# A two-layer block on one core: attention units in another order, the second feed-forward net by halves of the tokens, and LoRA masks made by matrix products

## The chip, the core and the metric

The kernel runs on one core of a Trainium2 chip. TensorE (PE in the rows) does matrix products and turns, VectorE (DVE), ScalarE (ACT) and GpSimd (POOL) work beside it, and SyncE (SP) issues nearly all transfers. Each engine runs its own list of instructions in the order in which it is written, and the lists meet in semaphores. The metric is the device time of one execution in microseconds (us).

## The reference, cut to what matters

There are 1024 tokens (32 sequences of 32) of width 256. The lines touched are those of the second layer and what follows it:

```python
x1 = _ln(x) * (1.0 + scale1) + shift1
qkv = (x1 @ qkv_w + qkv_b).reshape(Bc, Tc, 3, H, DH)      # 16 heads of 128
attn = softmax(einsum(q, k) * scale)                        # within a sequence of 32
x = x + gate1 * (einsum(attn, v) @ out_w + out_b)
x2 = _ln(x) * (1.0 + scale2) + shift2
h = jax.nn.gelu(x2 @ ffn_w1 + ffn_b1, approximate=False)   # width 1024
x = x + gate2 * (h @ ffn_w2 + ffn_b2)
# LoRA experts: 8 of rank 64, each token takes the best one
probs = softmax(x_flat @ Wr.T + br); expert_weight = max(probs)
h = einsum("nd,erd->ner", x_flat, A); y = einsum("ner,eor->neo", h, B) / 64
out = y[expert_idx] * expert_weight
```

The first layer (a convolution, a causal attention and a mixture of experts) comes ahead of it and is the same in both kernels.

## The kernel before, in words

Numbers in float32 are split into a high part and a low part, and a product of two of them is three matrix products (`split_mm`, lines 1397 to 1399). ScalarE makes the high part, and VectorE or GpSimd subtracts it from the whole to give the low part. The tokens are cut into 8 tiles of 128, and into 2 halves of 512 (c is the half, 0 or 1).

**Second attention.** The work is 8 units (j, c): j is a group of 4 heads, c a half of the tokens. For each, `proj1` makes queries, keys and values with 12 products (72 instructions), `scores1` the scores, VectorE the softmax, and one unit later `pv1` and `out1` the values and the output product of each of the 4 heads. The order is (0,0), (0,1), (1,0), (1,1), (2,0), (2,1), (3,0), (3,1). Each group has 4 pieces of weights (queries, keys, values, output), 16 in all, which go by SyncE into one of 4 raw buffers, by ScalarE (`piece_hi`, 128x1024) and GpSimd (`piece_lo`) into one of 6 slots. A piece is read in by the units of both halves.

**Between attention and the second net.** Since the last two units are (3,0) and (3,1), both halves of the output are complete only at the end. Then, for each half: VectorE adds the gated output to x (`residual2`), TensorE turns x into token rows (`turn_x2`, L1723), ScalarE copies it, VectorE normalises it, TensorE turns it back (`turn_z2`, L1740), VectorE applies scale and shift, and ScalarE and GpSimd split it. TensorE fills part of this time with turns of a constant that nobody reads (`keep_warm`, L1438): 22 ahead of the last `pv1`, 4, 8, 8 and 18 between the turns of half 0, and 14 behind the first product of the net.

**Second net.** 8 slices (m) of width 128, for each of the 2 halves: `ffn_up` (6 instructions) makes 128x512 of hidden values, ScalarE takes the Gelu (L933) and the high part (L937), VectorE the low part (`hidden_lo`, L1294), and `ffn_down` (6 instructions) adds to the output. The list `FFN` has three slices of half 0, three of half 1, two slices with both halves, and then three and three again. The weights of a slice go through one of 3 raw buffers (SyncE), `slice_hi` (ScalarE) and `slice_lo` (GpSimd).

**LoRA and the end.** When the net is done, x is complete and `logits1` gives the router's 8 logits (L1822). `lora_up` makes the hidden values of two experts at a time (8 products of 6 instructions, L1397 to L1399). The router's choice, with its share, is turned (`turn_sel`, L1830), copied by ScalarE, written to DRAM, and read back by SyncE so that each of 64 rows holds the mask of its expert. VectorE multiplies (L1379), `lora_down` (L1852) sums over experts, VectorE adds x (L1371), and 8 transfers write the output.

## Time and profile before

| | us |
|---|---|
| median of 3 runs | 650.28 |
| lowest and highest of the 3 | 649.84, 653.76 |
| the profiled execution, as timed | 652.73 |
| its span, first to last instruction | 650.6 |
| TensorE busy in it | 611.8 |

The profile is of one execution. Its span is 2.1 us less than its own time. A busy TensorE is not a TensorE that does useful work: the turns of `keep_warm` count as busy, and so does a product at the lower clock. In the timeline a group of like instructions is one row, and what stands in brackets is the idle time of the engine ahead of it and what ended it. A matrix product of 128x512 at the full clock is shown with 0.39 us, of which a part overlaps the next one: they start about 0.227 us apart.

### The profile page before, as it was taken

Reading aid. Unit: us, or ns where it says so; the run is one execution under the profiler, and the core shown is the slowest. Engines: PE = TensorE matmul, PEld = TensorE weight load, DVE = VectorE, ACT = ScalarE, POOL = GpSimd, SP = SyncE. Lnnn points to the kernel's source line nnn. Section 1 sums busy time; section 2 is a strip of 40 time slices with the busy share of each in tenths; the row PEclk is TensorE's granted clock in tenths of the full one; section 3 lists DMA queues with packets and bytes.
Section 4 is the critical chain, followed back from the end, with each engine's and each line's share of the span. In section 5 each row is a group of like instructions: output and inputs, shape, how many; then the busy total and the mean of one; then the engine's idle time right before and its main releaser. Section 6 shows DMA issues by size and latency. Waiting matters only on the chain.

```text
span 650.6 us, 13581 instructions
## 1 busy us (share of the span) xinstructions
PE 611.8 (94%) x5578; PEld 514.3 (79%) x5578; DVE 380.8 (59%) x672; ACT 339.2 (52%) x855; POOL 199.0 (31%) x214
## 2 busy tenths in 40 slices
PE   4679999999999999999899999999999999789997
PEld 1668888888888788888787887888888887668776
DVE  2689779777885665884844525153261437842553
ACT  2586677866876544542355553453544343445440
POOL 0566344354446314540333221040130013532000
PEclk9588999999999999999999999999999999989999
DMA  8460000000000247443002021020000002100023
GB/s 276 182 250 20 1 2 3 3 2 2 1 3 27 95 163 198 138 147 113 2 1 66 8 91 33 3 65 2 1 1 2 0 2 66 32 17 17 0 68 129
DMA packets 13101, 36.27 MB, mean 56 GB/s; under 512 B 2256, under 2 KB 3792, under 8 KB 12432
## 3 DMA queue, kind: packets, MB, share of 16 engines
q1 hardware_dynamic: 12800, 34.36, 16.2%
q10 hardware_dynamic: 240, 1.05, 0.6%
q8 instruction: 44, 0.72, 0.5%
q14 instruction: 17, 0.14, 0.1%
HBM read 34.29 MB, written 1.11 MB: 54 GB/s over the span
## 4 chain that ended last, share of the span: by engine, by line
PE 79%; DVE 11%; ACT 5%; issue 2%; DMA 2%; POOL 1%; SPq 0%; DVEq 0%; ACTq 0%
PE ps L1397 19%; PE ps L1398 18%; PE ps L1399 18%; PE ps L1515 7%; PE ps L1694 4%; PE ps L1474 2%; PE ps L1852 2%; DMA xT<-in_x_T 2%; ACT hid L671 2%; PE ps L1682 1%; PE ps L1504 1%; PE ps L1492 1%; PE ps L1426 1%; DVE strm_lo L1264 1%; ACT strm_hi L880 1%
## 5 line engine op out<-in xcount | busy, mean ns | idle before, releaser
L500 POOL TENSOR_TENSOR w_lo<-raw_w,w_hi 128x1024 fp32r<-128x1024 f32 x20 | 48.9, 2462 | 143.3 <-ACT w_hi L640 121.0
L1264 DVE SCALAR_TENSOR_TENSOR strm_lo<-ps,col,strm_hi 128x512 fp32r<-128x512 f32 x32 | 24.0, 751 | 113.9 <-ACT strm_hi L880 112.7
L1397 PE MATMUL ps<-w_hi,act_hi 128*128 128x512 f32 x160 | 65.7, 411 | 5.2 <-ACT junk L633 3.6
L864 ACT ACTIVATE work<-ps,col 128x512 f32<-128x512 f32 x64 | 44.2, 690 | 49.0 <-PE ps L1399 48.9
L1397 PE MATMUL ps<-act_hi,w_hi 128*128 128x512 f32 x160 | 62.9, 393 | 1.8 <-POOL act_lo L588 1.2
L1398 PE MATMUL ps<-w_lo,act_hi 128*128 128x512 f32 x160 | 63.6, 397 | 0.0
L1399 PE MATMUL ps<-w_hi,act_lo 128*128 128x512 f32 x160 | 63.4, 396 | 0.0
L1399 PE MATMUL ps<-act_hi,w_lo 128*128 128x512 f32 x160 | 62.3, 390 | 0.0
L1398 PE MATMUL ps<-act_lo,w_hi 128*128 128x512 f32 x160 | 62.3, 389 | 0.0
L1515 PE MATMUL ps<-raw_w,xT 128*128 128x256 f32 x256 | 61.3, 380 | 0.0
L1515 PEld LDWEIGHTS ps<-raw_w,xT 128*128 128x128 f32 x256 | 46.3, 190 | 5.3
L633 ACT ACTIVATE junk<-ps 128x128 f32<-128x128 f32 x160 | 43.9, 337 | 0.0
L1397 PE MATMUL ps<-act_hi,strm_hi 128*128 128x512 f32 x104 | 42.0, 404 | 0.0
L1398 PE MATMUL ps<-act_lo,strm_hi 128*128 128x512 f32 x104 | 41.4, 398 | 0.0
L1397 PEld LDWEIGHTS ps<-w_hi,act_hi 128*128 128x128 f32 x160 | 30.9, 193 | 13.2 <-issue 5.8
L1399 PE MATMUL ps<-act_hi,strm_lo 128*128 128x512 f32 x104 | 41.1, 395 | 0.0
L1397 PE MATMUL ps<-w_hi 128*128 128x256 f32 (+1 forms) x120 | 38.3, 319 | 2.3 <-DVE w_lo L1294 1.6
L633 ACT ACTIVATION_READ_ACCUMULATOR junk<-ps 128x1 f32 x160 | 40.0, 271 | 0.0
L1399 PE MATMUL ps<-w_hi,w_lo 128*128 128x256 f32 (+1 forms) x120 | 38.1, 317 | 0.0
L1398 PE MATMUL ps<-w_lo,w_hi 128*128 128x256 f32 (+1 forms) x120 | 37.9, 316 | 0.0
L714 ACT ACTIVATE work<-ps 128x512 f32<-128x512 f32 x40 | 24.1, 620 | 25.9 <-PE ps L1474 25.9
L1397 PEld LDWEIGHTS ps<-act_hi,w_hi 128*128 128x128 f32 x160 | 30.0, 188 | 8.3 <-issue 1.6
(192 smaller groups left out, 1458.4 us busy)
## 6 DMA issues: line engine op xcount, KB each, us to landing
raw_w<-in_w_attn SPq DMA_DIRECT2D x16, 512.0 KB, 4.2
raw_s<-in_w_moe SPq DMA_DIRECT2D x11, 384.0 KB, 5.5
work<-comb_dram SPq DMA_DIRECT2D x21, 128.0 KB, 2.9
raw_w<-in_w_qkv SPq DMA_DIRECT2D x4, 512.0 KB, 12.6
raw_w<-in_w_o SPq DMA_DIRECT2D x1, 2048.0 KB, 8.0
work<-comb_dram SPq DMA_DIRECT2D x8, 256.0 KB, 5.1
raw_s<-in_w_ffn SPq DMA_DIRECT2D x8, 256.0 KB, 2.6
bd<-in_w_ada SPq DMA_DIRECT2D x1, 1536.0 KB, 6.5
```

What stands on the lines that cost most here:

```text
L500: G.tensor_tensor(flat(w_lo[:, slot]), raw, flat(f32(w_hi[:, slot])), ALU.subtract).then_inc(s_piece_lo, 1)
L633: A(junk[:, squares[0] % 3, 0:n], src, ACT.Square, accum_out=total).then_inc(s_squares, 1)
L671: A(*conv_out(q, b, tiles), ACT.Copy).then_inc(s_y_act, 1)
L714: A(qkT[:, k * BANK:(k + 1) * BANK], ps[:, QK_BANK[k], :], ACT.Copy).then_inc(s_qkT_copied, 1)
L864: A(dst[:, h * BANK:(h + 1) * BANK], src, ACT.Identity, bias=c_(b, 4 * j + h)).then_inc(s_q1_copied, 1)
L1264: V.scalar_tensor_tensor(flat(strm_lo[:, n % SS]), ps[:, 4 + n % 2, :], c_("bv", 4 * (u // CHUNKS) + h), flat(f32(strm_hi[:, n % SS])), AL ...
L1397: mm(dst, ah, bh, start=start and i == 0, stop=False, **flags)
L1398: mm(dst, ah, bl, start=False, stop=False, **flags)
L1399: last = mm(dst, al, bh, start=False, stop=stop and i == len(terms) - 1, **flags)
L1474: last = nc.tensor.transpose(ps[:, QK_BANK[k], h * DH:(h + 1) * DH], qr[:, k * BANK + h * DH:k * BANK + (h + 1) * DH], ident)
L1515: mm(ps[:, 7, 0:D], attnT[:, h * P:(h + 1) * P], wo0[:, h, :], start=(h == 0), stop=(h == HQ - 1)).then_inc(s_o0_head, 1)
L1694: last = mm(ps[:, 4 + n % 2, t * P:(t + 1) * P], v1[:, u % 2, t, h * DH:(h + 1) * DH], bd[:, u % 2, 4 * h + t].rearrange("p b q -> p (b q) ...
```

## The change

The units of the attention are taken in the order (0,0), (0,1), (1,0), (1,1), (2,0), (3,0), (3,1), (2,1), so half 0 is complete one whole unit earlier. Group 2 is no longer done in one go, so its 4 pieces are loaded and split a second time (20 pieces instead of 16; `PIECES` is the first piece of a unit). The turns of half 0, its norm and its split are done beside the last unit's `proj1`, and the turned tiles lie in `hid`. `FFN` is now all slices of half 0 and then all of half 1. Two of its `ffn_up` stand ahead of the last unit's `pv1`, and the turns of half 1 stand among the products of half 0. The `keep_warm` calls there are gone, but for one of 8 turns between the halves. The first `logits1` stands within the second half of the net.

For the LoRA masks the transfers through DRAM are gone. VectorE writes once a constant of 8x128 for each pair of experts (`expand`), and a matrix product of it with the turned choice (`selT`) gives the mask in PSUM (`mask1`, one 128x512 instruction each, 8 in all). The share of the expert is now multiplied in where the result is added to x (`add_lora`, by tiles of 128 tokens).

TensorE, from the end of the loop over the units; before (L1438 is `keep_warm`, L1694 `pv1`, L1723 `turn_x2`, L1740 `turn_z2`):

```order
L1438 MATMUL ps<-cst 128x128 x22
L1694 MATMUL ps<-bd,work 128x128 [waits pv1_lo,bd1,q1_copied]
...
L1723 MATMUL ps<-cst,xT 128x128 [waits x2_ready,s1_shifted]
L1723 MATMUL ps<-cst,xT 128x128 x3
...
L1740 MATMUL ps<-cst,work 128x128 [waits z2_ready,q1_copied]
...
L1438 MATMUL ps<-cst 128x128 x4
```

and now (L1469 is the first instruction of a `split_mm`, those that read `strm_hi` belong to `out1` and those that read `act_hi` here to `ffn_up`; L1772 is `pv1`):

```order
L1469 MATMUL ps<-strm_hi,w_hi 128x512
...
L1469 MATMUL ps<-act_hi,w_hi 128x512 [waits xn3_ready,slice_lo]
...
L1469 MATMUL ps<-act_hi,w_hi 128x512 [waits s1_shifted,xn3_ready,slice_lo]
...
L1772 MATMUL ps<-bd,work 128x128 [waits pv1_lo,bd1,q1_copied]
...
L1772 MATMUL ps<-bd,work 128x128 [waits pv1_lo]
...
L1469 MATMUL ps<-strm_hi,w_hi 128x512 [waits acc1,piece_lo,pv1_lo]
...
L1772 MATMUL ps<-bd,work 128x128 [waits pv1_lo]
```

The filler is gone, and two products of the net stand ahead of the last unit's values.

TensorE, inside `proj1` of the last unit, now (L1813 is `turn_x2`, L1830 `turn_z2`; before there was nothing between the products here):

```order
L1469 MATMUL ps<-act_hi,w_hi 128x512 [waits q1_copied,piece_lo]
...
L1813 MATMUL ps<-cst,xT 128x128 [waits s1_shifted,x2_ready]
L1813 MATMUL ps<-cst,xT 128x128
L1469 MATMUL ps<-act_hi,w_hi 128x512 [waits q1_copied]
...
L1813 MATMUL ps<-cst,xT 128x128 [waits x2_ready]
...
L1469 MATMUL ps<-w_hi,act_hi 128x512 [waits q1_copied,piece_lo]
...
L1830 MATMUL ps<-cst,hid 128x128 [waits acc1,z2_ready]
L1830 MATMUL ps<-cst,hid 128x128
L1469 MATMUL ps<-w_hi,act_hi 128x512 [waits q1_copied]
```

The turns of half 0 stand ahead of the products 5 to 11, and the first waits for `x2_ready`, which VectorE gives.

ScalarE, behind the last exponent's unit, before (L647 is `slice_hi`, L880 the copy of `pv1`, L917 the copy of `turn_x2`):

```order
L647 ACTIVATE w_hi<-raw_s 128x512 [waits ld_slice0,out1,proj1]
...
L647 ACTIVATE w_hi<-raw_s 128x512 [waits ld_slice0]
L880 ACTIVATE strm_hi<-ps,col 128x512 [waits out1,pv1] x4
L917 ACTIVATE work<-ps 128x256 [waits x2T] x4
L647 ACTIVATE w_hi<-raw_s 128x512 [waits ld_slice1,out1]
L647 ACTIVATE w_hi<-raw_s 128x512 [waits ld_slice2]
...
L933 ACT_TABLE_LOAD
```

and now (L652 is `slice_hi`, L934 the Gelu, L944 the high part, L902 the copy of `pv1`):

```order
L950 ACT_TABLE_LOAD
...
L652 ACTIVATE w_hi<-raw_s 128x512 [waits ld_slice2,proj1]
L652 ACTIVATE w_hi<-raw_s 128x512 [waits ld_slice0]
L652 ACTIVATE w_hi<-raw_s 128x512 [waits ld_slice1]
L652 ACTIVATE w_hi<-raw_s 128x512 [waits ld_slice2]
L934 ACTIVATE work<-ps,col 128x512 [waits ffn_up]
L944 ACTIVATE w_hi<-work 128x512 [waits out1,gelu]
L902 ACTIVATE strm_hi<-ps,col 128x512 [waits out1,pv1] x2
```

The copies of the last unit's `pv1` stood behind four slices before. Now the table load, four slices, the first Gelu and its high part stand ahead of the first two of them.

The diff, cut to its core:

```diff
         g32 = v1_[:, 0:2 * BANK].rearrange("p (r n) -> p r n", r=2)
-        cb1 = work[:, 0:4 * TOK].rearrange("p (r n) -> p r n", r=MR)
         h1 = bd[:].rearrange("p r a b c -> p (r a b c)").rearrange("p (r n) -> p r n", n=BANK)
 
+        selT = w_hi2[0:NE, 2:4, :]
...
@@ -337,7 +339,11 @@
         QK_BANK = (2, 3, 0, 1, 2)
         Y_FIRST, Y_REST = slice(0, 2), slice(2, TILES)
         U = GROUPS * CHUNKS
-        NP1 = 4 * GROUPS
+        UNITS = ((0, 0), (0, 1), (1, 0), (1, 1), (2, 0), (3, 0), (3, 1), (2, 1))
+        PIECES = (0, 0, 4, 4, 8, 12, 12, 16)
+        LAST_UNIT = (1, 3, 4, 6)
+        NP1 = 4 * GROUPS + 4
+        C0_DONE = 6
         NM = CHUNKS * MI
         NF = CHUNKS * MM
...
         Z_BEHIND = (4, 6, 8, 10)
 
-        FFN = ([(m, c) for c in range(CHUNKS) for m in range(SS)]
-               + [(m, c) for m in range(SS, MM - SS) for c in range(CHUNKS)]
-               + [(m, c) for c in range(CHUNKS) for m in range(MM - SS, MM)])
+        FFN = [(m, c) for c in range(CHUNKS) for m in range(MM)]
+        SLICE_SLOT = (2, 4, 5, 0)
+        HIDDEN = (6, 7, 2, 3)
+        Z2_BANK = (6, 7, 3, 6, 6, 7, 6, 7)
+        X2_BEHIND = (5, 6, 7, 8)
+        Z2_BEHIND = (9, 10, 11)
+
+        def up_bank(n):
+            return 3 - n % 2 if n < MM else 4 + n % 4
+
...
-            u = CHUNKS * j + CHUNKS - 1
+            u = LAST_UNIT[j]
...
+                sp.dma_start(raw_p[:, i % RAWS, :], w_attn1[i if i < 4 * GROUPS else i - 8]).then_inc(ld_piece[i % RAWS], 16)
...
-            for c in range(CHUNKS):
-
-                s = slice(c * BANK, (c + 1) * BANK)
-                sp.wait_ge(s_selT_ready, c + 1)
-                sp.dma_start(comb_dram[1, :, s], selT[0:NE, s]).then_inc(st_comb, 16)
-                sp.wait_ge(st_comb, 16 * (CHUNKS + c + 1))
-                for n in range(c * MR, (c + 1) * MR):
-                    m = LORA[n][0]
-                    spread(cb1[:, m, s], 1, m, RANK, ld_cb1[n], s)
             for t in range(TILES):
-                sp.wait_ge(s_y_ready, t // 2 + 1)
+                sp.wait_ge(s_y_ready, t + 1)
...
                 piece_lo(NPROJ + i, raw_p[:, i % RAWS, :], i % WSLOTS)
-            def mod2(c):
+            for f in range(2):
+                slice_lo(MI + f, f, 4)
+            for c in range(CHUNKS):
                 for t in range(c * CT, (c + 1) * CT):
                     pool.wait_ge(s_ln2st, t + 1)
                     inv_root(stat[:, 40 + t:41 + t], bst[:, t, 7:8], 1, 1.0, 1e-6, s_l2rstd)
                 for t in range(c * CT, (c + 1) * CT):
                     mod_lo(TILES + t, t, mt2[:, t % 4, :], s_xn3_ready)
-
-            for f in range(4):
-                slice_lo(MI + f, f, 4)
-            mod2(0)
-            slice_lo(MI + 4, 4, 4)
-            slice_lo(MI + 5, 5, 4)
-            mod2(1)
-            for f in range(6, MM):
-                slice_lo(MI + f, f, 4)
+                if c == 0:
+                    for f in range(2, MM):
+                        slice_lo(MI + f, f, 4)
...
+                    if u == U - 1:
+                        if k in (2, 3):
+                            act.wait_ge(s_proj1, 12 * (U - 1))
+                            slice_hi(MI + k - 2, k - 2, 4)
+                        if k in X2_BEHIND:
+                            take_x2(X2_BEHIND.index(k))
+                        if k in Z2_BEHIND[1:]:
+                            mod2_hi(Z2_BEHIND.index(k) - 1)
...
+            TAKEN = ((), (6, 7, 8), (9,), (10, 11, 12), (13, 14, 15), (16, 17), (18, 19), ())
...
+                for i in TAKEN[u]:
+                    used_sem, count = piece_free(i)
+                    act.wait_ge(used_sem, count)
+                    piece_hi(NPROJ + i, i % RAWS, i % WSLOTS)
...
+            A(junk[:, 0, 0:1], half[:, 0:1], ACT.Gelu)
+            act.wait_ge(s_proj1, 12 * U)
+            for f in range(2, 6):
+                slice_hi(MI + f, f, 4)
+            take_ffn(0)
+            take_pv1(U - 1, (0, 1))
+            take_ffn(1)
+            take_pv1(U - 1, (2, 3))
+            for f in range(6, MM):
+                slice_hi(MI + f, f, 4)
+            take_ffn(2)
+            take_ffn(3)
+            for t in range(CT, TILES):
+                take_x2(t)
+            take_ffn(4)
+            take_ffn(5)
...
-
-            x4_hi(0)
+                act.wait_ge(s_ffn_down, NF)
+                A(selT[:, c, :], ps[0:NE, c, :], ACT.Copy).then_inc(s_selT_ready, 1)
...
-                dve.wait_ge(s_acc1, DK * (U - CHUNKS + c + 1))
+                dve.wait_ge(s_acc1, DK * (C0_DONE if c == 0 else U))
...
+                if u == C0_DONE:
+                    residual2(0, range(DK))
+                    for t in range(CT + 2):
+                        if t < CT:
+                            stats2(t)
+                        if 1 <= t <= CT:
+                            apply2(t - 1)
+                        if t >= 2:
+                            modulate2(t - 2)
+            hidden_lo(0)
+            low_heads(U - 1, (0, 1))
+            hidden_lo(1)
+            low_heads(U - 1, (2, 3))
+            add_out(U - 1)
             residual2(1, range(DK))
-            norm2(1)
-
-            for n in range(2, NF):
-                hidden_lo(n)
-
-            def router1(c):
+            stats2(4)
+            stats2(5)
+            hidden_lo(2)
+            apply2(4)
+            stats2(6)
+            apply2(5)
+            hidden_lo(3)
+            stats2(7)
+            apply2(6)
+            modulate2(4)
+            apply2(7)
+            modulate2(5)
+            modulate2(6)
+            hidden_lo(4)
+            modulate2(7)
...
+            def end_ffn(c):
+                dve.wait_ge(s_ffn_down, MM * (c + 1))
                 for m in range(DK):
                     gated(ps[:, 2 * c + m, :], 5, "b2", c, m).then_inc(s_x4_ready, 1)
...
+            for n in range(5, NF):
+                hidden_lo(n)
+                if n == MM:
+                    dve.wait_ge(s_out1, 4 * U)
+                    for m in range(MR):
+                        V.tensor_copy(expand(m).rearrange("p (e r) -> p e r", e=2),
+                                      over(ident[0:NE, 2 * m:2 * m + 2], RANK)).then_inc(s_expand, 1)
+                if n == MM + 1:
+                    end_ffn(0)
+                if n == MM + 3:
+                    x4_lo(0)
+                if n == MM + 6:
+                    router_shift(0)
+            router_probs(0)
+            end_ffn(1)
+            router_pick(0)
+            x4_lo(1)
+            router_shift(1)
+            router_probs(1)
+            router_pick(1)
+
...
-                for a in range(c * CT // 2, (c + 1) * CT // 2):
-                    t2 = slice(2 * a, 2 * a + 2)
-                    V.tensor_tensor(xres[:, t2, :], ps[:, (a + 2) % 4, :].rearrange("p (b n) -> p b n", b=2),
-                                    xres[:, t2, :], ALU.add).then_inc(s_y_ready, 1)
+                dve.wait_ge(s_share, c + 1)
+                for t in range(c * CT, (c + 1) * CT):
+                    V.scalar_tensor_tensor(xres[:, t, :], ps[:, (t // 2 + 2) % 4, (t % 2) * D:(t % 2 + 1) * D],
+                                           rt[:, 6, t, 0:1], xres[:, t, :], ALU.mult, ALU.add).then_inc(s_y_ready, 1)
...
-                dve.wait_ge(ld_cb1[n], 32)
+                dve.wait_ge(s_mask1, n + 1)
                 if n >= 3:
                     dve.wait_ge(s_hmk_used, n - 2)
-                V.tensor_tensor(hmk[:, n % 3, :], h1[:, n, :], cb1[:, m, c * BANK:(c + 1) * BANK],
+                V.tensor_tensor(hmk[:, n % 3, :], h1[:, n, :], ps[:, 4 + n % 4, :],
...
+                    if u == U - 1 and k in X2_BEHIND:
+                        turn_x2(X2_BEHIND.index(k))
+                    if u == U - 1 and k in Z2_BEHIND:
+                        turn_z2(Z2_BEHIND.index(k))
                     n = 12 * u + k
-                    i = 4 * j + k // 4
+                    i = PIECES[u] + k // 4
...
-            def turn_x2(c):
-                pe.wait_ge(s_x2_ready, DK * (c + 1))
...
+            ffn_up(0)
+            ffn_up(1)
+            pv1(U - 1, 0)
+            pv1(U - 1, 1)
+            out1(U - 1, 0)
+            pv1(U - 1, 2)
+            out1(U - 1, 1)
+            pv1(U - 1, 3)
+            out1(U - 1, 2)
+            out1(U - 1, 3)
+            ffn_up(2)
+            ffn_down(0)
+            ffn_up(3)
+            turn_x2(4)
+            turn_x2(5)
+            ffn_down(1)
+            turn_x2(6)
+            turn_x2(7)
+            ffn_up(4)
+            ffn_down(2)
+            turn_z2(4)
+            turn_z2(5)
+            ffn_up(5)
+            ffn_down(3)
+            turn_z2(6)
+            turn_z2(7)
+            ffn_up(6)
+            ffn_down(4)
+            ffn_up(7)
+            ffn_down(5)
+            ffn_down(6)
+            ffn_down(7)
+            keep_warm(8, 5)
+            ffn_up(8)
+            ffn_up(9)
+            for n in range(10, NF):
+                ffn_up(n)
+                ffn_down(n - 2)
+                if n == NF - 3:
+                    logits1(0)
+            ffn_down(NF - 2)
+            ffn_down(NF - 1)
+
...
+            def mask1(n):
+                m, c = LORA[n]
+                if n == 0:
+                    pe.wait_ge(s_expand, MR)
+                pe.wait_ge(s_selT_ready, c + 1)
+                pe.wait_ge(s_up_copied, MR + n % MR + 1)
+                if c == 1:
+                    pe.wait_ge(s_hmk_ready, n - MR + 1)
+                mm(ps[:, 4 + n % 4, :], expand(m), selT[:, c, :],
+                   start=True, stop=True).then_inc(s_mask1, 1)
 
...
             for n in range(NL):
                 if n == 2:
                     logits1(1)
-                if n == 3:
+                if n == MR:
                     turn_sel(0)
-                if n == MR + 1:
-                    turn_sel(1)
                 lora_up(n)
-            for n in range(MR):
-                lora_down(n)
-            pe.wait_ge(s_selT_ready, CHUNKS)
-            for n in range(MR, NL):
+                if n >= NL - 2:
+                    mask1(n - NL + 2)
+            turn_sel(1)
+            mask1(2)
+            lora_down(0)
+            mask1(3)
+            for n in range(1, NL):
+                if n + MR - 1 < NL:
+                    mask1(n + MR - 1)
                 lora_down(n)
 
```

## Rows read from the trace of the kernel before

**Rows 1.** The page: busy time, share of the span, instructions.
```profile
PE 611.8 (94%) x5578; PEld 514.3 (79%) x5578; DVE 380.8 (59%) x672; ACT 339.2 (52%) x855; POOL 199.0 (31%) x214
```
**Rows 2.** Timeline, TensorE, 509 to 574: start, duration, line, tiles, count, [idle <-releaser].
```profile
509.54 0.40 PE L1397 MATMUL ps<-act_hi,w_hi 128*128 128x512 f32 x1
...
536.85 2.56 PE L1438 MATMUL ps<-cst 128*128 128x128 f32 x22
...
540.00 2.02 PE L1694 MATMUL ps<-bd,work 128*128 128x128 f32 x16 [0.58 <-issue]
...
542.69 0.50 PE L1397 MATMUL ps<-strm_hi,w_hi 128*128 128x512 f32 x1 [0.67 <-DVE strm_lo L1264]
...
551.71 0.41 PE L1740 MATMUL ps<-cst,work 128*128 128x128 f32 x2
...
558.73 0.47 PE L1397 MATMUL ps<-act_hi,w_hi 128*128 128x512 f32 x1 [0.62 <-POOL act_lo L588]
...
563.50 0.66 PE L1723 MATMUL ps<-cst,xT 128*128 128x128 f32 x4 [1.62 <-DVE xT L1283]
...
570.14 0.44 PE L1740 MATMUL ps<-cst,work 128*128 128x128 f32 x2 [0.69 <-DVE work L1218]
...
572.13 0.50 PE L1397 MATMUL ps<-w_hi 128*128 128x512 f32 x1 [1.55 <-DVE w_lo L1294]
...
573.20 0.63 PE L1397 MATMUL ps<-w_hi 128*128 128x512 f32 x1
```
**Rows 3.** Timeline, TensorE, from the dense second feed-forward net to the end.
```profile
576.58 0.39 PE L1397 MATMUL ps<-act_hi,w_hi 128*128 128x512 f32 x1
...
613.07 0.39 PE L1399 MATMUL ps<-w_hi,w_lo 128*128 128x512 f32 x1
...
614.33 1.95 PE L1822 MATMUL ps<-r_w,xT 128*128 128x8 f32 x16 [0.87 <-DVE xT L1283]
...
617.28 0.63 PE L1398 MATMUL ps<-act_lo,strm_hi 128*128 128x512 f32 x1
...
627.59 0.60 PE L1830 MATMUL ps<-cst,rt 128*8 128x128 f32 x4 [0.51 <-DVE rt L1350]
...
632.14 13.97 PE L1852 MATMUL ps<-raw_s,work 128*128 128x256 f32 x64
```
**Rows 4.** Timeline, VectorE, the attention units and behind the last.
```profile
426.48 2.28 DVE L1064 TENSOR_TENSOR sm_e<-sm_e,sm_r 128x512 f32<-128x512 f32 x1
...
509.63 2.90 DVE L1078 STREAM_TRANSPOSE bd<-sm_e 32x512 f32<-32x512 f32 x4
...
512.56 1.29 DVE L1275 TENSOR_TENSOR yT<-ps,yT 128x512 f32<-128x512 f32 x2
...
558.54 1.84 DVE L1281 SCALAR_TENSOR_TENSOR yT<-yT,col,ada 128x512 f32<-128x512 f32 x1
...
561.98 0.74 DVE L1281 SCALAR_TENSOR_TENSOR yT<-yT,col,ada 128x512 f32<-128x512 f32 x1
```
**Rows 5.** Timeline, GpSimd, in the same two stretches.
```profile
425.80 7.57 POOL L500 TENSOR_TENSOR w_lo<-raw_w,w_hi 128x1024 fp32r<-128x1024 f32 x3 [22.63 <-ACT w_hi L640]
...
558.54 2.97 POOL L507 TENSOR_TENSOR w_lo<-raw_s,w_hi 128x512 fp32r<-128x512 f32 x2
```
**Rows 6.** Timeline, ScalarE, the attention units and behind the last.
```profile
454.99 1.06 ACT L640 ACTIVATE w_hi<-raw_w 128x1024 fp32r<-128x1024 f32 x1 [2.53 <-PE ps L1399]
...
539.00 0.63 ACT L647 ACTIVATE w_hi<-raw_s 128x512 fp32r<-128x512 f32 x1 [2.92 <-DMA raw_s<-in_w_ffn]
...
565.57 1.28 ACT L933 ACT_TABLE_LOAD   x1
```
**Rows 7.** Timeline, SyncE's queue.
```profile
536.44 23.75 SPq L468 DMA_DIRECT2D raw_s<-in_w_ffn  x5
```
**Rows 8.** Groups by line and shape, 340 to the end: busy, mean ns, idle before.
```profile
L1379 DVE TENSOR_TENSOR work<-bd,work 128x512 f32<-128x512 f32 x8 | 5.5, 692 | 8.6 <-DMA work<-comb_dram 8.1 <-ACT bd L963 0.5
...
L933 ACT ACTIVATE work<-ps,col 128x512 f32<-128x512 f32 x16 | 11.0, 688 | 18.7 <-PE ps L1399 16.7 <-DVE w_lo L1294 2.0
```

More of the change, by code:

```diff
@@ L331, in build_program @@
         s_wsel = sem("wsel")
+        s_expand = sem("expand")
+        s_share = sem("share")
         s_hmk_ready = sem("hmk_ready")
@@ new lines, in _ @@
+            pe.wait_ge(s_x1_ready, 1)
+            for t in range(CT):
+                keep_warm((14, 14, 6, 14)[t], 0)
+                turn_z(t)
+            keep_warm(16, 0)
+            pe.wait_ge(s_x1_ready, 2)
+            for u in range(U):
+                proj1(u)
+                if u == 1:
+                    pe.wait_ge(s_xn1_ready, TILES)
+                    pe.wait_ge(s_xT1_copied, TILES)
+                if u == U - 1:
+                    turn_z2(CT - 1)
+                if u >= 1:
+                    pv1(u - 1, 0)
+                    pv1(u - 1, 1)
+                if u == 0:
+                    pe.wait_ge(s_x1_ready, 4)
+                scores1(u)
+                if u >= 1:
+                    out1(u - 1, 0)
+                    pv1(u - 1, 2)
+                    out1(u - 1, 1)
+                    pv1(u - 1, 3)
+                    out1(u - 1, 2)
+                    out1(u - 1, 3)
```

354 lines of the change are left out of this document (150 added, 204 removed).

## The prediction

> **What bounds the kernel now.** I read the page's busy times first. TensorE is busy for 611.8 of 650.6 us [rows 1], so it sets the pace, and a gain must come from time in which it waits, turns a filler, or runs at its lower clock. The timeline of TensorE was next. Ahead of 536.85 each unit of the attention takes 27.3 us without a gap worth naming: the last unit's `proj1` starts at 509.54 and the filler behind that pass of the loop at 536.85 [rows 2]. The second net is dense from 576.58 to 613.3; between the rows 576.58 and 613.07 lie 161 steps, 0.227 us each [rows 3], so a `split_mm` of 6 instructions is 1.36 us. Between 536.85 and 576.58, and around 614, the time is not dense, and the change works there. ScalarE, VectorE, GpSimd and SyncE are read only for what they would make TensorE wait for.
>
> **What goes.** All in TensorE's time:
> - the 22 filler turns and the idle time behind them, 536.85 to 540.00: 3.15. The wait ahead of 542.69: 0.7 [rows 2].
> - 551.71 to 558.73 is 7.0, in which the four tiles of `turn_z2` are work, 0.25 each (a filler turn is 2.56 / 22 = 0.12 and a tile takes two): 6.0 goes [rows 2].
> - the first `ffn_up` of 558.73 ends its six steps at 560.1, and the turn behind it starts at 563.50: 3.4 [rows 2].
> - 563.50 to 572.13 is 8.6; two `ffn_up` (2.7), four `turn_x2` tiles at 0.33 (two are 0.66) and four `turn_z2` tiles are work, 5.0 together: 3.6 goes [rows 2].
> - the lower clock behind this: 572.13 to 576.58 holds 12 steps and takes 4.45 instead of 2.7. A product of 128x512 is 0.63 there and 0.39 when dense [rows 2, 3], so the granted clock is at its lower level of 1.2 GHz, after a stretch in which TensorE waited for 0.69 and 1.55 with only turns around it: 1.7.
> - ahead of the LoRA part 0.9 of idle time at 614.33, and the same dip after it (0.63 again at 617.28): 1.7. Now the first `logits1` stands inside the net, where it costs what it cost (it only moves). The wait ahead of the second turned choice at 627.59: 0.5 [rows 3].
>
> Together 21.7. The turns of half 0, four of each kind, move and cost the same.
>
> **What comes.**
> - 8 mask products of 128x512, single instructions, 8 x 0.227 = 1.8. Filler of 8 turns: 0.9.
> - The mask transfers bring nothing back. VectorE waits for them for 8.1 us in sum [rows 8], but from 614.33 on TensorE's only idle time is the 0.5 counted above, and the 64 records of `lora_down` run for 13.97 without a break [rows 3]. The share moves from a multiply at the router to the last sum, which becomes 8 instructions of 256 columns for 4 of 512: nothing on the path beyond some tenths.
> - Between units 4 and 5 ScalarE now has three pieces in a row (13, 14, 15), and the first waits for the end of `out1`, as the piece at 454.99 did (1.06 each, released by TensorE) [rows 6]. 3.2 of pieces and 0.69 for the first copy put the third product of `proj1` off to 4.0 from 2.7: 1.3.
> - **The first turn of half 0** stands ahead of product 5 of the last `proj1`, at 6.8 behind its start S. VectorE must by then have ended the turns of the softmax (509.63 and 2.90) and `add_out` (512.56 and 1.29), which is S + 4.3 [rows 2, 4], and then two pairs of `residual2`. A pair is 0.74 and about 0.69 (the mean of L1379, of the same size), so both are 2.9 and ready at S + 7.2: a stall of 0.4, the low end. But GpSimd now splits pieces 18 and 19 (about 2.5 each, three are 7.57) and slices 0 and 1 at that time. With GpSimd at work the softmax product at 426.48 took 2.28, and `residual2` at 558.54 took 1.84 where it takes 0.74 alone [rows 4, 5]. If all of it is stretched so (1.6, and 2.0 for a pair), it is ready at S + 10.8: 4.0, the high end. Slice 1 is done by about S + 6.8, soon after `residual2` starts at S + 5.9 (4.3 and the first stretch of 1.6), so I take the first stretch whole and a third of the second: 2.7.
>
>   The Trainium skill ("SBUF — State Buffer", section on SBUF's two separate sides) states that VectorE with two SBUF inputs and GpSimd hold a shared port for a whole instruction and the other blocks. By that rule the stall would be the rest of slice 1 and no more, 2.7 again and not 4.0, and a stretch by a factor, as the bare rows could be read, would give 4.0. The rows fit it: 558.54 is the start of both.
> - **Behind the last pass**, at E. ScalarE loads its table (1.28 at 565.57), which now is at E - 2.3 to E - 1.0, and then takes slices 2 to 5, before the copies of `pv1`. Slice 5 needs a buffer that GpSimd frees by slice 2, near E + 1.1, and a transfer, which took 2.56 from the issue at 536.44 to its use at 539.00 [rows 6, 7]: E + 3.7. With the copy of slice 5 (0.63), the Gelu (0.69), its high part (0.63) and the copy of `pv1` (0.69) ScalarE is at E + 6.3, and VectorE's low part at E + 7.1 [rows 6, 8]. TensorE has two `ffn_up` (2.7) and two `pv1` (2.0) to do until E + 4.7: 2.4 of idle time. At the low end, with the slice in time, it is 0.3.
> - These two stalls stand where TensorE is otherwise dense. Each is longer than the 1.55 that had a dip behind it, and the fillers are gone. I count one dip of 1.7 for the two (none to two are the ends).
> - Handing over among turns, `residual2` of half 1 and the low parts: VectorE has about 15 us of work in a row there against some 14 of products, and each low part is ready 0.5 to 2 us before it is needed by my count: 1.0.
>
> Sum: 1.8 + 0.9 + 1.3 + 2.7 + 2.4 + 1.7 + 1.0 = 11.8 come and 21.7 go: -9.9. The profiled execution would go from 652.7 to 642.8 (span 640.7). It lay 2.4 above the median of the runs, so the median would be 650.3 - 9.9 = **640.4**.
>
> **Rivals.**
> 1. *The new waits are covered.* The piece, the residual and the slice are in time or nearly (low ends: 1.3 less 0.8, 2.7 less 2.3, 2.4 less 2.1) and no dip follows (1.7): 640.4 - 6.9 = 633.5. For it: with piece 19 split earlier than I think VectorE runs alone, and 4 us between S and the first turn are then nearly enough. Against it: the pairs of rows 4 and 5. Chance 0.18.
> 2. *VectorE becomes late throughout the first half of the net.* Two dips, the residual at its high end and 3 more of waiting for low parts: 640.4 + 1.7 + 1.3 + 3 = 646.4. For it: the order puts norms ahead of the low parts. Chance 0.14.
> 3. *The masks do give back their wait*: if the LoRA part is held by VectorE's 8.1 us, it is 632. Against it stands the unbroken row of 13.97. Chance 0.02.
> 4. *Slower*: the first half of the net falls into step with its Gelu. Only two banks serve its `ffn_up`, so when a low part comes later than its `ffn_down`, product n + 2 waits for n as well, and each of the 8 slices pays Gelu, high and low part one behind the other: 0.69 + 0.63 + 0.69 + 0.2 for handing on = 2.2, 17.6 in sum: 658. It decides once VectorE is more than a slice (2.7) behind; my count leaves 0.7 ahead at the third low part. Chance 0.04.
>
> The forecast has 0.62. **Range** 633.5 to 647: it reaches rival 1 and rival 2, and leaves out rivals 3 and 4 and the tails, under 0.2. A change of less than 1% (6.5 us, so 643.8 to 656.8) can't be told from none here. The forecast with nearly all of its chance, and rivals 1 and 3, are faster by more: 0.86; rival 2 and the forecast's upper tail are within: 0.10; rival 4 slower: 0.04.
>
> **What would show it.** In the changed profile: no `keep_warm` of 22, the span about 10 shorter. An idle time of 1 to 1.5 ahead of the third product of unit 5's `proj1`, released by ScalarE. One of 2 to 3 ahead of the first `turn_x2`, released by VectorE's xT; if it is 0.5, rival 1. About 2.4 ahead of the last unit's first `out1`, released by the low part; behind one of them some products at 0.63. A net of some 60 us from the end of the loop to its last product. `lora_down` without waits for masks. I am wrong if TensorE waits within the net for `w_lo` again and again, or if a stall sits where I named none: the first places to look are the pieces 16 to 19 and the buffers of the slices.

## The result

| | before | changed |
|---|---|---|
| median of 14 runs each, us | 652.84 | 647.75 |
| lowest and highest | 649.84, 655.25 | 641.88, 651.39 |
| the profiled execution, as timed | 652.73 | 647.96 |
| its span | 650.6 | 646.2 |

The ratio is 0.9909 (95% interval 0.9884 to 0.9934): 0.9% faster, 5.1 us on the medians, where 9.9 was forecast. That is less than the 1% which was said to be hard to tell from none, but the interval leaves 1 out. 647.75 lies 0.75 above the range. Part of the distance to 640.4 is the base: the median of the three runs shown was 650.28, that of all 14 is 652.84. The rest, 4.8 us, is a matter of the kernel.

The first line of the changed kernel's page answers to [rows 1]. TensorE is busy for 3.4 us less, and still for 94% of the span:

```profile
PE 608.4 (94%) x5520; PEld 509.0 (79%) x5520; DVE 381.9 (59%) x680; ACT 342.0 (53%) x860; POOL 207.9 (32%) x218
```

TensorE's timeline of the changed kernel, the waits and what follows them. L1469 to L1471 are the three products of a `split_mm`, L1813 is `turn_x2`, L1800 `logits1`. A stretch of products shown with 0.63 for 0.39 is called a *dip* from here on: TensorE's granted clock is at its lower level in it.

```profile
459.52 0.50 PE L1469 MATMUL ps<-act_hi,w_hi 128*128 128x512 f32 x1 [0.90 <-ACT work L884]
...
521.54 0.64 PE L1813 MATMUL ps<-cst,xT 128*128 128x128 f32 x2 [2.61 <-DVE xT L1322]
...
522.41 0.63 PE L1470 MATMUL ps<-act_lo,w_hi 128*128 128x512 f32 x1
...
552.76 0.50 PE L1469 MATMUL ps<-strm_hi,w_hi 128*128 128x512 f32 x1 [2.04 <-DVE strm_lo L1303]
...
576.14 0.50 PE L1469 MATMUL ps<-w_hi 128*128 128x512 f32 x1 [0.78 <-DVE w_lo L1333]
...
610.78 1.95 PE L1800 MATMUL ps<-r_w,xT 128*128 128x8 f32 x16 [0.31 <-DVE xT L1322]
...
613.85 0.63 PE L1471 MATMUL ps<-act_hi,strm_lo 128*128 128x512 f32 x1
```

All three forecast waits are there, with the releasers forecast and nearly the sizes: 0.90 (I had 1.3), 2.61 (2.7), 2.04 (2.4). What had gone in the old region (the 22 fillers, the waits and turns of [rows 2]) is gone. What is missing from the gain is at the end. `mask1` is L1958 and `lora_down` L1968; TensorE's timeline, then its weight loads (PEld) of the first two rows:

```profile
621.36 0.39 PE L1471 MATMUL ps<-act_hi,strm_lo 128*128 128x512 f32 x1
621.68 0.50 PE L1958 MATMUL ps<-w_hi,strm_hi 8*128 8x512 f32 x1
622.11 0.50 PE L1469 MATMUL ps<-act_hi,strm_hi 128*128 128x512 f32 x1
622.44 0.39 PE L1470 MATMUL ps<-act_lo,strm_hi 128*128 128x512 f32 x1
...
627.00 0.73 PE L1958 MATMUL ps<-w_hi,strm_hi 8*128 8x512 f32 x2
627.66 2.00 PE L1968 MATMUL ps<-raw_s,work 128*128 128x256 f32 x8
629.59 0.50 PE L1958 MATMUL ps<-w_hi,strm_hi 8*128 8x512 f32 x1
630.01 2.00 PE L1968 MATMUL ps<-raw_s,work 128*128 128x256 f32 x8
631.94 0.50 PE L1958 MATMUL ps<-w_hi,strm_hi 8*128 8x512 f32 x1
...
634.71 7.17 PE L1968 MATMUL ps<-raw_s,work 128*128 128x256 f32 x32
```

```profile
621.14 0.19 PEld L1471 LDWEIGHTS ps<-act_hi,strm_lo 128*128 128x128 f32 x1
621.68 0.18 PEld L1958 LDWEIGHTS ps<-w_hi,strm_hi 8*128 8x128 f32 x1 [0.35 <-issue]
622.10 0.19 PEld L1469 LDWEIGHTS ps<-act_hi,strm_hi 128*128 128x128 f32 x1 [0.25 <-issue]
```

Read the starts, not the durations. Two products of 128 rows start 0.227 us apart. Here the mask product starts 0.32 after the one ahead of it, the next one 0.43 after it, and the one behind that 0.33 later: 1.08 for three steps that take 0.68 elsewhere, so 0.40 more. And the weight load of a 128-row product runs 0.22 ahead of its product (621.14 for 621.36), while that of the mask product starts with it, and so does the next one. A mask with its eight `lora_down` takes 2.35 (629.59 to 631.94), where eight alone take 1.74 (64 take 13.97 in [rows 3]). The masks were forecast at 0.227 each.

### The profile page after: what moved, and what is told of

Read it like the earlier page. It is cut to its first block, busy times and chain, and to the rows that moved or that the text cites. A ratio compares the mean times of both kernels' runs of the same rounds, so it can differ in the third digit from the quotient of the medians.

```text
span 646.2 us, 13493 instructions
## 1 busy us (share of the span) xinstructions
PE 608.4 (94%) x5520; PEld 509.0 (79%) x5520; DVE 381.9 (59%) x680; ACT 342.0 (53%) x860; POOL 207.9 (32%) x218
## 3 DMA queue, kind: packets, MB, share of 16 engines
HBM read 34.29 MB, written 1.08 MB: 55 GB/s over the span
## 4 chain that ended last, share of the span: by engine, by line
PE 81%; DVE 8%; ACT 5%; issue 2%; DMA 2%; POOL 1%; SPq 0%; DVEq 0%; ACTq 0%
PE ps L1469 19%; PE ps L1471 18%; PE ps L1470 18%; PE ps L1587 7%; PE ps L1772 4%; PE ps L1546 3%; PE ps L1968 2%; DMA xT<-in_x_T 2%; PE ps L1564 2%; ACT hid L676 2%; PE ps L1760 1%; PE ps L1576 1%; PE ps L1623 1%; DVE strm_lo L1303 1%; PE ps L1498 1%
## 5 line engine op out<-in xcount | busy, mean ns | idle before, releaser
L509 POOL TENSOR_TENSOR w_lo<-raw_w,w_hi 128x1024 fp32r<-128x1024 f32 x24 | 58.5, 2457 | 160.7 <-ACT w_hi L645 139.0
L1303 DVE SCALAR_TENSOR_TENSOR strm_lo<-ps,col,strm_hi 128x512 fp32r<-128x512 f32 x32 | 23.9, 750 | 103.1 <-ACT strm_hi L902 102.1
L1469 PE MATMUL ps<-w_hi,act_hi 128*128 128x512 f32 x160 | 66.3, 414 | 4.6 <-ACT junk L638 3.2
L1469 PE MATMUL ps<-act_hi,w_hi 128*128 128x512 f32 x160 | 64.2, 401 | 2.0 <-ACT work L884 0.9
L1471 PE MATMUL ps<-w_hi,act_lo 128*128 128x512 f32 x160 | 63.8, 399 | 0.0
L1471 PE MATMUL ps<-act_hi,w_lo 128*128 128x512 f32 x160 | 62.9, 393 | 0.0
L1469 PE MATMUL ps<-act_hi,strm_hi 128*128 128x512 f32 x104 | 41.8, 402 | 0.0
L1471 PE MATMUL ps<-act_hi,strm_lo 128*128 128x512 f32 x104 | 41.3, 397 | 0.0
L1469 PEld LDWEIGHTS ps<-w_hi,act_hi 128*128 128x128 f32 x160 | 31.0, 194 | 12.4 <-issue 5.4
L1469 PE MATMUL ps<-w_hi 128*128 128x256 f32 (+1 forms) x120 | 37.8, 315 | 1.5 <-DVE w_lo L1333 0.8
L1471 PE MATMUL ps<-w_hi,w_lo 128*128 128x256 f32 (+1 forms) x120 | 37.4, 312 | 0.0
L1469 PEld LDWEIGHTS ps<-act_hi,w_hi 128*128 128x128 f32 x160 | 30.5, 191 | 8.7 <-ACT work L884 1.3
```

The lines of the kernel that those rows point to most:

```text
L509: G.tensor_tensor(flat(w_lo[:, slot]), raw, flat(f32(w_hi[:, slot])), ALU.subtract).then_inc(s_piece_lo, 1)
L1303: V.scalar_tensor_tensor(flat(strm_lo[:, n % SS]), ps[:, 4 + n % 2, :], c_("bv", 4 * UNITS[u][0] + h), flat(f32(strm_hi[:, n % SS])), ALU. ...
L1469: mm(dst, ah, bh, start=start and i == 0, stop=False, **flags)
L1471: last = mm(dst, al, bh, start=False, stop=stop and i == len(terms) - 1, **flags)
```

## The experiments

Each was timed in turn with the kernel before on one chip, and ratios are against that. There were three sets: the kernel before had 654.82, 654.18 and 653.73 in them. In the first set the question was where the missing 4.8 us are: A, in the masks; B, in the reordering.

**The masks alone, in the kernel before.**

```
-                dve.wait_ge(ld_cb1[n], 32)
+                dve.wait_ge(s_mask1, n + 1)
...
-                V.tensor_tensor(hmk[:, n % 3, :], h1[:, n, :], cb1[:, m, c * BANK:(c + 1) * BANK],
+                V.tensor_tensor(hmk[:, n % 3, :], h1[:, n, :], ps[:, 4 + n % 4, :],
```

> The kernel before with one part of the change alone: masks by 8 products, share at the last sum; the order of units and of the net as before. Theory A (a mask product costs 0.63 on TensorE, product and changeover, as the spacing of 0.43 plus a longer lora_down beside it in the changed kernel's trace suggests): 8 x 0.63 = 5.0 more, 0.5 of waiting for the second choice less, so 4 to 5 us slower than the kernel before. Theory B (it costs its 0.23, as predicted, and the LoRA part of the changed kernel is long only by its dip in the clock): 1 to 2 us slower. Rival C (the mask transfers did hold the LoRA part): faster by 3 or more.

657.21 us, ratio 1.0037 (1.0008 to 1.0067): 2.4 us slower, with the interval from 0.5 to 4.4. In its trace a mask product starts 0.42 ahead of its successor, as in the changed kernel (0.43):

```profile
631.23 0.50 PE L1850 MATMUL ps<-w_hi,strm_hi 8*128 8x512 f32 x1
631.65 0.50 PE L1394 MATMUL ps<-act_hi,strm_hi 128*128 128x512 f32 x1
```

From the first `logits1` to the end of the last `lora_down` it takes 35.62 (615.80 to 644.25 + 7.17) where the kernel before takes 31.78 (614.33 to 646.11): 3.84 longer. So the mask half of the change is a loss by itself, on the time as well, though the time lies between the two theories (A: 4 to 5 slower, B: 1 to 2).

**The transfers back, in the changed kernel.**

```
+                sp.dma_start(comb_dram[1, :, s], selT[0:NE, s]).then_inc(st_comb, 16)
...
+                    spread(cb1[:, m, s], 1, m, RANK, ld_cb1[n], s)
...
-                mm(ps[:, 4 + n % 4, :], expand(m), selT[:, c, :],
-                   start=True, stop=True).then_inc(s_mask1, 1)
```

> The changed kernel with the masks sent through DRAM again; all else of the change kept. Theory A: the 5.0 of the products go, and the transfers cost some 2 of waiting, since the choice is turned no earlier against the products: 2 to 4 us faster than the changed kernel, ratio to before near 0.987. Theory B: 1.8 go and 2 of waiting come: the same as the changed kernel. Rival C: slower than the changed kernel by 3 or more, lora_down held by the transfers.

644.80 us, ratio 0.9845 (0.9806 to 0.9884). The transfers are the better way against masks of 8 rows, though TensorE now does wait for VectorE twice:

```profile
623.64 7.17 PE L1961 MATMUL ps<-raw_s,work 128*128 128x256 f32 x32 [0.66 <-DVE work L1455]
631.27 7.14 PE L1961 MATMUL ps<-raw_s,work 128*128 128x256 f32 x32 [0.45 <-DVE work L1455]
```

These 1.1 us are all that VectorE's waits for transfers are worth to TensorE: 8.6 us in this trace (8.1 in [rows 8]).

**Mask products over 128 rows.** The 8 rows are padded by rows of zeros that lie there anyway; the number of products, their columns and their order stay.

```
-        selT = w_hi2[0:NE, 2:4, :]
-        expand = lambda m: strm_hi[0:NE, m // 2, 2 + m % 2, :]
+        selT = w_hi2[:, 2:4, :]
+        expand = lambda m: strm_hi[:, m // 2, 2 + m % 2, :]
...
```

> The changed kernel with the mask products summed over 128 rows of which 120 are zeros, instead of over 8 rows. If the changeover between an 8-row product and the 128-row ones around it is what costs (A1), the spacing from a mask to the next product falls from 0.43 to about 0.23 to 0.3 and the kernel is 2 to 3 us faster than the changed one. If the cost lies in going between the single-instruction format and the two-record float32 products (A2), spacing and time stay as they are.

642.66 us, ratio 0.9830 (0.9787 to 0.9872). Sixteen times as many rows, and it is faster. TensorE's timeline and its loads:

```profile
618.45 0.39 PE L1471 MATMUL ps<-act_hi,strm_lo 128*128 128x512 f32 x1
618.67 0.39 PE L1958 MATMUL ps<-w_hi,strm_hi 128*128 128x512 f32 x1
618.90 0.39 PE L1469 MATMUL ps<-act_hi,strm_hi 128*128 128x512 f32 x1
...
624.87 0.58 PE L1958 MATMUL ps<-w_hi,strm_hi 128*128 128x512 f32 x1
625.29 1.89 PE L1968 MATMUL ps<-raw_s,work 128*128 128x256 f32 x8
626.83 0.58 PE L1958 MATMUL ps<-w_hi,strm_hi 128*128 128x512 f32 x1
```

```profile
618.45 0.19 PEld L1958 LDWEIGHTS ps<-w_hi,strm_hi 128*128 128x128 f32 x1
618.68 0.19 PEld L1469 LDWEIGHTS ps<-act_hi,strm_hi 128*128 128x128 f32 x1
```

Now the load is at 618.45 for the product at 618.67, and a mask costs 0.227, or 1.95 with its eight `lora_down` (624.87 to 626.83). So it isn't the product that is slow, it is the change between 8 and 128 rows. From 0.991 to 0.983 is more than the rows account for: some 5 us, of which the masks are 2.7 (the table below). This trace also lacks the dip behind the first turn; the rest lies within the intervals.

**Other row counts**, 32 and 64, one execution each and read from the trace alone (`w_hi2[0:32, ...]` and `w_hi2[0:64, ...]` in the lines above).

> The changed kernel with the mask products over 32 rows (24 of them zero) instead of 8. Read from the trace alone, since one time says nothing here. Theory A1 (any product that uses fewer than the 128 rows pays when its row count differs from its neighbour's): the distance from a mask product to the next instruction stays 0.43 us and the group of 8 lora_down behind it about 1.93. Theory A2 (only very few rows are slow, for instance because the operands come from few partitions): the distance is between 0.43 and 0.227.

> The same over 64 rows (56 of them zero). A1: again 0.43 us and 1.93. A2: nearer to 0.227 than with 32 rows.

With 64 rows the picture is that of 8, to the hundredth, and with 32 too (0.43 from 626.68 to 627.11):

```profile
621.20 0.39 PE L1471 MATMUL ps<-act_hi,strm_lo 128*128 128x512 f32 x1
621.52 0.50 PE L1958 MATMUL ps<-w_hi,strm_hi 64*128 64x512 f32 x1
621.95 0.50 PE L1469 MATMUL ps<-act_hi,strm_hi 128*128 128x512 f32 x1
```

A1 holds: any of the row counts 8, 32 and 64 pays the same among products of 128.

**Filler in the two late places.**

```
+                    if u == U - 1 and k == X2_BEHIND[0]:
+                        keep_warm(22, 3)
                     if u == U - 1 and k in X2_BEHIND:
                         turn_x2(X2_BEHIND.index(k))
...
             pv1(U - 1, 1)
+            pe.wait_ge(s_q1_copied, 12 * U)
+            keep_warm(16, 0)
             out1(U - 1, 0)
```

> The changed kernel with 22 filler turns ahead of the first turn of x2 in the last proj1 and 16 ahead of the last unit's first out1, in the two places where TensorE waits 2.61 and 2.04 in its trace. If the dip in the clock behind 521.8 comes of that wait (theory D), it is gone in the trace (no 128x512 product of 0.63 there), and the time is 1 to 2 us under the changed kernel's. If dips come by themselves (rival E), there is one all the same and the time is the same.

646.05 us, ratio 0.9867 (0.9828 to 0.9906). TensorE has no product at the lower clock anywhere behind the start of the attention in this execution. The filler stands in the time of the waits and ends neither sooner. So I put the gain, about 3 us against the changed kernel, down to the dips: behind the two waits there are 1.3 of them on average (counted below), about 2.1 us. The interval is too wide to tell 2.1 from 3.

**The changed kernel once more**, in the second set.

> The changed kernel once more, with nothing edited, beside the others of this set, so that they can be compared on one chip. Both theories: 0.991 of the kernel before, as in the first comparison (interval 0.988 to 0.993), so about 649 us if the kernel before is again at 654.8. In its trace the rows of the attention and of the LoRA part as before: first turn_x2 2.6 us late, out1 of the last unit 2.0 late, each mask product of 8 rows 0.43 us ahead of the next instruction. Whether a stretch at the lower clock (0.63 us per 128x512 product) follows the late turn and the second logits may differ: in the five traces so far it followed the late turn in 2 of 4 and the logits in 4 of 6.

649.75 us, ratio 0.9915 (0.9887 to 0.9943). In this execution there are dips in three places, one more than in the first: 5 rows at 0.63 behind the first turn, 3 behind the last unit's first `out1`, 7 behind `logits1`.

**Slice 5 later on ScalarE.**

```
-            for f in range(2, 6):
+            for f in range(2, 5):
                 slice_hi(MI + f, f, 4)
             take_ffn(0)
             take_pv1(U - 1, (0, 1))
+            slice_hi(MI + 5, 5, 4)
             take_ffn(1)
```

> The changed kernel, ScalarE's split of slice 5 moved behind the copies of the last unit's first two pv1. Theory A (the 2.04 us ahead of the last unit's first out1 come from slice 5, whose transfer ends late and which stands ahead of the copy on ScalarE): the first copy starts at about 1 us behind the first pv1, the low part 0.7 later, and the idle time falls to 0.8 or less: 1.2 to 1.5 us shorter than the changed kernel, about 0.989. Rival B (VectorE's own list, Gelu low parts and turns of the softmax, holds the low part): the idle time stays at 2 and the time too, 0.991.

643.69 us, ratio 0.9828 (0.9797 to 0.9858). The wait is 0.67 now:

```profile
552.13 0.50 PE L1470 MATMUL ps<-strm_hi,w_hi 128*128 128x512 f32 x1 [0.67 <-DVE strm_lo L1304]
```

From the last `pv1` to the second `logits1` it takes 60.69 (549.43 to 610.12), the first execution of the changed kernel 62.08 (548.70 to 610.78) without a dip there, and the second 63.73 (550.17 to 613.90) with one. So 1.39 is the wait, as theory A said, and 1.65 is the dip, which the shorter wait did not show. The medians differ by 6.1, more than those two. The profiled execution has no dip behind `logits1` either (1.6), and the mean granted clock is 0.979 over the five executions, for 0.969 over the six of the changed kernel beside it, which points to fewer dips in this version. Why the one behind `logits1` would be rarer is open.

**The turns of half 0 two products later.**

```
-        X2_BEHIND = (5, 6, 7, 8)
-        Z2_BEHIND = (9, 10, 11)
+        X2_BEHIND = (7, 8, 9, 10)
+        Z2_BEHIND = (11,)
...
```

The other three `turn_z2` go behind `proj1`, among `pv1(6, 0)` and `pv1(6, 1)`.

> The changed kernel, the four turn_x2 of half 0 two products later in the last proj1 (ahead of products 7 to 10 instead of 5 to 8), turn_z2 0 ahead of product 11 and the other three behind proj1 and among the two pv1. Theory A (the residual is ready 9.45 us behind the start of this proj1, two products later the turn finds it ready): the 2.6 us ahead of the first turn go, 0.5 to 1.5 come back behind it, since VectorE starts the softmax of the last unit later by so much: 1 to 2 us shorter than the changed kernel, and the stretch at the lower clock that followed in 2 of 4 traces (1.7 us) not there: 0.987 to 0.989. Rival B (the norm is the bound up to the end of the loop): the same 2.6 us show up ahead of out1 or pv1 instead: 0.991.

645.29 us, ratio 0.9860 (0.9832 to 0.9887). The first turn waits for nothing any more; half of it comes back one step on, where `out1` waits for the norm's last step:

```profile
535.64 0.47 PE L1475 MATMUL ps<-strm_hi,w_hi 128*128 128x512 f32 x1 [1.25 <-DVE work L1273]
```

Between the same two points (511.37 to 546.58) it takes 35.21 and the changed kernel beside it 38.26 (511.91 to 550.17): 1.4 less waiting and one dip less.

**All mends together**: 128 rows, slice 5, the turns, and the fourth weight piece of group 3 taken inside the next `proj1` instead of as the third in a row.

```
+                    if u == 5 and k == 3:
...
+                        piece_hi(NPROJ + 15, 15 % RAWS, 15 % WSLOTS)
...
-            TAKEN = ((), (6, 7, 8), (9,), (10, 11, 12), (13, 14, 15), (16, 17), (18, 19), ())
+            TAKEN = ((), (6, 7, 8), (9,), (10, 11, 12), (13, 14), (16, 17), (18, 19), ())
```

> The changed kernel with every mend at once: mask products over 128 rows (120 of them zero), slice 5 later, the turns of half 0 later, and the fourth weight piece of group 3 taken inside the next proj1 instead of as the third of three in a row (its 0.9 us of idle time ahead of the third product go). If the parts add up: 2.7 (masks) + 1.3 + 1.5 + 0.9 = 6.4 us less than the changed kernel, and about one stretch at the lower clock less: 0.979 to 0.982 of the kernel before. If the masks' width was not the cause of what was measured before (0.983), no better than 0.985.

640.15 us, ratio 0.9767 (0.9737 to 0.9796), 9.6 us less than the changed kernel beside it. More than the 6.4 of the parts and one dip, 8.1, though within the intervals.

**And the second logits in two parts**, with the former once more beside it in the third set:

```
-                if n == 2:
-                    logits1(1)
+                if n in (2, 3):
+                    logits1(1, 2 * (n - 2), 2 * (n - 1))
...
                 lora_up(n)
```

The two numbers added to `logits1` are the first tile and the one behind the last.

> The version with all four mends once more, with nothing edited, beside the next one: 0.977 of the kernel before (interval 0.974 to 0.980 at first).

> The version with all four mends, and logits1 of half 1 in two parts of 8 short products, with one lora_up between them. Theory D (the stretch at the lower clock behind it, 1.7 us in 7 of 10 traces, comes from TensorE having 0.3 us of idle time and 1.8 us of short products in a row): the stretch is gone or rarer, 0.5 to 1.7 us less than the version with four mends, the choice of half 1 comes 1.4 us later and still in time (it was ready 2.7 early). Rival (it comes whatever stands there): the stretch shows in the trace as before, no difference.

639.18 us, ratio 0.9770 (0.9738 to 0.9802), and 637.32 us, ratio 0.9747 (0.9718 to 0.9776). The wait of 0.31 stays and no dip follows: none of the products between the two parts and behind them is at 0.63.

```profile
606.10 1.06 PE L1811 MATMUL ps<-r_w,xT 128*128 128x8 f32 x8 [0.31 <-DVE xT L1331]
...
608.26 0.39 PE L1482 MATMUL ps<-act_hi,strm_lo 128*128 128x512 f32 x1
608.50 0.95 PE L1811 MATMUL ps<-r_w,xT 128*128 128x8 f32 x8
```

The medians differ by 1.9, the size of a dip, with intervals that overlap. One trace without the dip shows little (3 of 11 had none with `logits1` in one piece), but the mean granted clocks point the same way: 0.981 on average over these six executions, and 0.976 over the twelve with the four mends alone. This last version beats both kernels: 2.5% less than before.

**The LoRA part over all traces.** One length settles the two terms: from the start of the second `logits1` to the end of the last `lora_down`. A dip is seen by 6 to 8 rows at 0.63.

| mask products | dip | traces | us | one of them |
|---|---|---|---|---|
| 8, 32 or 64 rows | yes | 5 | 31.06 to 31.10 | 610.78 to 641.88, the changed kernel |
| 8 rows | no | 2 | 29.48, 29.51 | 609.67 to 639.15, with filler |
| 128 rows | yes | 3 | 28.37 to 28.39 | 606.65 to 635.02, all mends |
| 128 rows | no | 1 | 26.79 | 606.10 to 632.89, logits in two |
| transfers | no | 1 | 26.58 | 611.83 to 638.41 |

The four corners fit one another: changing rows costs 2.7 with a dip (31.07 less 28.37) and 2.7 without (29.49 less 26.79), and a dip costs 1.6 with either. The masks alone in the kernel before fit too: 1.8 and 2.7, less the wait of 0.5 that goes, are 4.0, and 3.84 was measured. And the last two rows say what the mask products are worth: with 8 rows they cost 2.9 more than the transfers, and with 128 rows still 0.2 more, in one trace each. No version of them was shown to beat the transfers.

## Why the prediction was wrong

The direction was right, and the reordering half came in full: from the first product of the attention to the last of the net it takes 281.6 us (325.74 to 607.37) for 289.3 (323.75 to 613.07), 7.7 less, where the terms of the prediction give 6.9 less with the first `logits1` (1.7) moved in. From there to the last `lora_down` it takes 34.5 for 33.0: 1.5 more, where 3.0 less was forecast. Two terms in this part were wrong. Against the profiled execution (652.73 to 647.96, so -4.8 where -9.9 was forecast) 5.1 is missing.

- **The step that failed: "8 mask products of 128x512, single instructions, 8 x 0.227 = 1.8".** They measure 4.5: the table's 2.7 on top of 1.8, which is about 0.40 for each of the 7 places where rows change (629.59 to 631.94 is 2.35, less the 1.95 with 128 rows), the two masks in a row counting once (0.66 for both at 627.00). I took the price from the shape of the output and never looked at "8x512", nor at the weight loads, which have lines of their own. The trace of before had the answer. In the first layer a product of 32 rows (L1504) stands among those of 128, and the starts are 0.32 apart, with the load not ahead:

```profile
82.53 0.39 PE L1399 MATMUL ps<-w_hi,act_lo 128*128 128x512 f32 x1
82.85 1.17 PE L1504 MATMUL ps<-pT,work 32*128 32x128 f32 x32
83.95 0.50 PE L1397 MATMUL ps<-w_hi,act_hi 128*128 128x512 f32 x1
```

```profile
82.85 0.98 PEld L1504 LDWEIGHTS ps<-pT,work 32*128 32x128 f32 x32 [0.35 <-issue]
```

  The Trainium skill ("TensorE: Matmul & The Clock Gate", the section on loading the stationary operand) states that the time of a weight load goes by its columns and not by its rows. The rows agree: 0.18 for 8x128, 0.19 for 128x128. So the cost isn't in the load's length; what goes with it is the load's place.
- **The second step that failed: "ahead of the LoRA part 0.9 of idle time at 614.33, and the same dip after it: 1.7".** The dip was counted as gone. The idle time is gone but for 0.31, the dip isn't. It moved to the second `logits1`, which waits only 0.31 and is then 1.8 us of products with 8 columns. Of the 11 traces of the changed kernel and its variants with `logits1` in one piece 8 have the dip: 1.6 missing in the profile. With the logits in two parts it was gone in the one trace there is.
- **2.0 us lie ahead of all that was changed**: the first product of the attention starts at 325.74 here and at 323.75 in the profile of before. Executions differ so in this stretch with one and the same program: in other traces of the changed kernel's variants, which are equal up to there, that product starts at 323.54 to 327.23, and at 325.23 in the kernel before with the masks alone. TensorE's clock goes with it: up to this product it is at the lower level for 27.3 us in the changed kernel's profile, for 23.9 in that of before and in the one that starts at 323.54. So these 2.0 us belong to the pair of executions and not to the kernel.
- **The waits that come** were a little smaller than forecast (0.4, 0.1 and 0.4), which gives back 0.9. Hand-overs within the net: 0.78 at 576.14 and the 0.31 above, for 1.0. 2.7 + 1.6 + 2.0 - 0.9 is 5.4, against 5.1.
- **For the medians** 4.8 is missing. The masks are 2.7, the dip behind `logits1` 1.2 on average (8 of 11), the dips behind the two waits 0.4 more than the 1.7 counted, and the smaller waits give back 0.9: 3.4. The other 1.4 is open; the interval of the ratio is 3.3 us wide.
- **The first turn at 2.7** came out at 2.61, where the bare stretch by a factor would have given 4.0. VectorE's two operations beside GpSimd, in its timeline:

```profile
511.33 2.27 DVE L1099 TENSOR_TENSOR sm_e<-sm_e,sm_r 128x512 f32<-128x512 f32 x1
513.64 2.91 DVE L1113 STREAM_TRANSPOSE bd<-sm_e 32x512 f32<-32x512 f32 x4
...
517.90 1.47 DVE L1320 SCALAR_TENSOR_TENSOR yT<-yT,col,ada 128x512 f32<-128x512 f32 x1
519.41 0.69 DVE L1322 TENSOR_TENSOR xT<-xT,yT 128x512 f32<-128x512 f32 x1
520.02 0.74 DVE L1320 SCALAR_TENSOR_TENSOR yT<-yT,col,ada 128x512 f32<-128x512 f32 x1
```

```profile
510.65 5.22 POOL L509 TENSOR_TENSOR w_lo<-raw_w,w_hi 128x1024 fp32r<-128x1024 f32 x2 [22.10 <-ACT w_hi L645]
516.17 2.65 POOL L516 TENSOR_TENSOR w_lo<-raw_s,w_hi 128x512 fp32r<-128x512 f32 x2 [0.30 <-ACT w_hi L652]
```

  The same operation takes 1.47 while GpSimd's slice runs until 518.82, and 0.74 at 520.02 when it doesn't; the turns with one input take 2.91 as always. One operation is held in each of the two stretches, not all of them, and both end 0.55 behind the end of the GpSimd instruction that ran when they began: at 513.60 behind 513.05 (the first of the two at 510.65 takes 2.40), and at 519.37 behind 518.82. They lost 1.6 and 0.7, as the sum had it. By the rule cited ahead (the Trainium skill, "SBUF — State Buffer", on SBUF's two separate sides) that is so, and the trace agrees.
- **One dip for the two waits.** A dip follows the wait of 2.6 in 6 of 7 traces and the wait of 2.0 in 3 of 7, so 1.3 on average. One came in the profile, which is luck as much as reckoning, and is a little low for the median.
- **The rivals.** Rival 2 had a time near the result (646.4) and not its mechanism: VectorE is not late in the net but for 0.78. Rival 3 would have needed the transfers to hold TensorE; putting them back costs 1.1 of waiting and gains time all the same. Rival 4's falling into step didn't happen, and rival 1's covered waits didn't either. The chances were added up wrongly: the forecast with rivals 1 and 3 has 0.82 at most and not 0.86, and rival 2 alone has 0.14, more than the 0.10 given to a change within 1%. The result fell there.

## What to carry to other kernels

Price an added product by its neighbours as well as by its own size: compare its number of contraction rows with theirs, look at the weight-load rows of a like place, and pad with zeros to the common count if that is free. A wait of 2 us in an otherwise dense TensorE costs itself and, in 9 of the 14 cases here, a dip of about 1.6. Count dips as chances over several traces, not as facts of one. And a transfer whose result an idle engine waits for is worth what the busy engine waits for that engine (here 1.1 of 8.6 us), so weigh that against what its replacement puts on the busy one.
